# In step zero, VectorE instead of ScalarE copies queries, keys and kept rows out of PSUM

## What is computed

```python
def _adj_from_feats(Xa, W1, W2, W3):
    Q = Xa @ W1
    K = Xa @ W3
    logits = Q @ W2 @ K.T / TAU
    idx = jnp.argsort(-logits, axis=1)
    ...
    keep_sorted = ranks < k_i[:, None]      # k_i: entries until the sum passes 0.9
    ...
    masked = jnp.where(keep, logits, -jnp.inf)
    return jax.nn.softmax(masked, axis=1)
for s in range(STEPS):                       # STEPS = 2
    A = _adj_from_feats(Xa, W1, W2, W3)
    Xf = Rf @ Xf
    Xb = Rb @ Xb
    Xa = A @ Xa
    Z = Z + (Xf @ U1[s] + Xb @ U2[s] + Xa @ U3[s])
Y = X + Z
```

## Time and profile before

| what | us |
|---|---|
| three runs: median (lowest, highest) | 2160.16 (2159.7, 2162.64) |
| profiled execution: time, and its span | 2161.51, 2159.80 |
| busy in the span: PE, PEld | 1879.6, 1255.7 |
| busy in the span: DVE, ACT, POOL | 1911.5, 1681.3, 945.7 |
| mean granted TensorE clock, as a share of 2.4 GHz | 0.953 |

### The profile page before, as it was taken

One profiled execution on the slowest core, in us unless ns is written; L12 is line 12 of the kernel. 1 busy time (PEld: TensorE's weight loads), 2 busy tenths in 40 slices (PEclk: granted clock), 3 DMA queues, 4 the chain that ended last, 5 costly groups with the idle time before them and its releaser, 6 DMA issues. The chain is left out here.

```text
span 2159.8 us, 32672 instructions
## 1 busy us (share of the span) xinstructions
PE 1879.6 (87%) x9866; PEld 1255.7 (58%) x9866; DVE 1911.5 (89%) x6117; ACT 1681.3 (78%) x1740; POOL 945.7 (44%) x1542
## 2 busy tenths in 40 slices
PE   3999765999999999999973999989998999899892
PEld 2565433666666666666641656565656666565662
DVE  7788888999999999999748999999999999999995
ACT  5444256999999999999626898999998998999840
POOL 2000054666666666666605344443444344434424
PEclk9999987999999999999996999999999999999996
DMA  7788330111111111111116010101010010101023
GB/s 263 294 317 312 119 131 20 34 55 51 56 56 40 49 55 51 56 56 50 40 64 220 1 45 23 45 23 45 23 44 24 26 42 23 45 23 45 22 95 122
DMA packets 65727, 167.62 MB, mean 78 GB/s; under 512 B 7037, under 2 KB 45307, under 8 KB 61947
## 3 DMA queue, kind: packets, MB, share of 16 engines
q1 hardware_dynamic: 65530, 165.43, 22.1%
HBM read 117.95 MB, written 47.45 MB: 77 GB/s over the span
## 5 line engine op out<-in xcount | busy, mean ns | idle before, releaser
L1474 PE MATMUL banks<-xa,pt 128*128 128x256 f32 x2704 | 642.7, 389 | 7.6 <-ACT pt L974 7.6
L1474 PEld LDWEIGHTS banks<-xa,pt 128*128 128x128 f32 x2704 | 507.7, 194 | 146.6 <-issue 71.3
L946 ACT ACTIVATE junk_a<-pb_all,minus_t 128x3327 f16<-128x3327 f32 x150 | 460.7, 3071 | 73.8 <-POOLq L866 71.6
L950 ACT ACTIVATE junk_a<-pb_all,minus_t 128x3327 f16<-128x3327 f32 x150 | 460.6, 3071 | 4.1
L1525 PE MATMUL banks<-region,at 128*128 128x512 f16 x2028 | 456.1, 380 | 0.0
L850 POOL TENSOR_SCALAR over<-over,target 128x1 f32<-128x1 f32 x150 | 219.3, 1462 | 269.8 <-ACT junk_a L946 267.3
L1525 PEld LDWEIGHTS banks<-region,at 128*128 128x128 f16 x2028 | 196.6, 98 | 218.0 <-issue 2.0
L1400 PE MATMUL banks<-keys,qs 64*128 64x512 f32 (+1 forms) x816 | 192.0, 568 | 91.7 <-DMA qs<-q_d 31.9
L974 ACT ACTIVATE pt<-banks 128x896 f32<-128x896 f32 x208 | 173.2, 859 | 75.1 <-PE banks L1466 74.2
L1266 DVE TENSOR_SCALAR_CACHE_REDUCE pb_all<-banks 128x1024 f32<-128x1024 f32 x260 | 209.2, 848 | 21.3 <-PE banks L1400 13.0
L1128 DVE MAX8 junk_v<-below 128x8 f32<-128x208 f32 (+1 forms) x624 | 222.4, 432 | 2.2
(11 more groups left out here) (224 smaller groups left out, 2835.0 us busy)
## 6 DMA issues: line engine op xcount, KB each, us to landing
at<-adjT_d SPq DMA_DIRECT2D x52, 832.0 KB, 4.8
region<-in_adj_dram SPq DMA_DIRECT2D x25, 1663.5 KB, 7.9
adjT_d<-at SPq DMA_DIRECT2D x26, 832.0 KB, 3.9
fb_d<-fb_sb SPq DMA_DIRECT2D x26, 256.0 KB, 2.0
region<-fb_d SPq DMA_DIRECT2D x2, 3328.0 KB, 19.2
y_d<-y_sb SPq DMA_DIRECT2D x50, 128.0 KB, 1.7
x_d<-pb_all SPq DMA_DIRECT2D x1, 3328.0 KB, 10.4
qs<-q_d SPq DMA_DIRECT2D x104, 32.0 KB, 4.1
```

The costliest lines, as they stand in the source:

```text
L946: nc.scalar.activation(junk_a[:, 0:w], pb[u][:, 0:w], ACT.Relu, scale=sign, bias=t, accum_out=over[u][:, a:a + 1])\
L950: nc.scalar.activation(junk_a[:, 0:w], pb[u][:, 0:w], ACT.Sign, scale=sign, bias=t, accum_out=over[u][:, 2 + a:3 + a])\
L1474: last = nc.tensor.matmul(bank[4][:, 0:D], pt[sl][:, t * P:(t + 1) * P], xa[:, t0 + t, :], start=(t0 + t == 0), stop=(t0 + t == T - 1))
```

## The change

Step one is untouched. In step zero three things move from ScalarE to VectorE. The copies of queries and keys (ScalarE's `queries_keys`, behind its last copy of transposed pieces) go into `add_z`, behind the sum of z. With this `add_z` no longer waits for `qk_done`, and its first copy waits for the store of `qo` of the tile before. The kept rows of tile i - 1 become `kept_rows(i - 1)`, between the release of `unsettled` and the masking pass of tile i; for the last tile they stand in VectorE's iteration for i = 26, in front of the takes of step one's first scores. TensorE's, POOL's and SP's orders are as before.

```diff
@@ ScalarE, body(i) @@
-                    def queries_keys(q):
-
-                        act.wait_ge(S("z_psum"), q.n + 1)
-                        act.wait_ge(S("qo_stored"), 16 * q.n)
-                        nc.scalar.activation(qo[:, :], bank[7][0:DA, D:D + P], ACT.Copy)
-                        nc.scalar.activation(key_tiles(1, q.t, 1), bank[7][DA:2 * DA, D:D + P], ACT.Copy)\
-                            .then_inc(S("qk_done"), 1)
-
...
-                        if first and c == NT - 1 and (k + -1).inside(T):
-                            queries_keys(k + -1)
...
-                    if k.inside(T):
+                    if not first and k.inside(T):
 
                         sl, use = k.ring(NT, NT - 1)
                         act.wait_ge(S2("pt_used")[sl], use + 1)
-                        if first:
-                            act.wait_ge(S2("xo_stored")[k.slot], 16 * k.use)
                         nc.scalar.activation(xo_sb[k.slot][:, :], bank[4][:, 0:D], ACT.Copy, scale=rkept[k.slot][:, :])\
                             .then_inc(S2("xo")[k.slot], 1)
@@ VectorE, search(i) @@
                     dve.sem_inc(S("unsettled"), 1)
                     if first:
+                        kept_rows(i + -1)
                         ch.add(nc.vector.scalar_tensor_tensor(out=p, in0=p, scalar=left_max[:, :], in1=p, op0=ALU.is_gt, op1=ALU.mult))
@@ VectorE, add_z(k) @@
                         dve.wait_ge(S("z_psum"), k.n + 1)
-                        dve.wait_ge(S("qk_done"), k.n + 1)
                         dve.wait_ge(S2("y_stored")[k.slot], 16 * k.use)
                         nc.vector.tensor_tensor(y_sb[k.slot][:, :], bank[7][:, 0:D], xa[:, k.t, :], ALU.add).then_inc(S2("y_done")[k.slot], 1)
+                        dve.wait_ge(S("qo_stored"), 16 * k.n)
+                        nc.vector.tensor_copy(qo[:, :], bank[7][0:DA, D:D + P])
+                        nc.vector.tensor_copy(key_tiles(1, k.t, 1), bank[7][DA:2 * DA, D:D + P]).then_inc(S("qk_done"), 1)
...
+                def kept_rows(k):
+
+                    if not k.inside(T):
+                        return
+                    sl, use = k.ring(NT, NT - 1)
+                    dve.wait_ge(S2("pt_used")[sl], use + 1)
+                    dve.wait_ge(S2("xo_stored")[k.slot], 16 * k.use)
+                    nc.vector.tensor_scalar(xo_sb[k.slot][:, :], bank[4][:, 0:D], rkept[k.slot][:, :], None, ALU.mult)\
+                        .then_inc(S2("xo")[k.slot], 1)
@@ VectorE, body(i), iterations 26 and 27 @@
                         spread(i + -1)
                         add_z(i + -2)
+                        if first:
+                            kept_rows(i + -1)
                         if first and i.t == T:
                             take_logits(nxt, 0, 3)
```

## The result

The changed kernel takes **2188.46 us** in the median of four runs (2184.68 to 2190.25), against 2159.93 us for the kernel before on the same chip (2159.01 to 2162.64). The ratio is 1.0128, 95% interval 1.011 to 1.0145: slower by 1.3%. The forecast was 2176.3 us with a range up to 2184, so the sign was right and the size was not: +28.5 us where the sum said +16.1. The profiled execution has a time of 2188.08 and a span of 2186.4 us, 26.6 us over the 2159.8 of before.

The account below looks back on a forecast made before the run. VectorE was taken to bound step zero's tiles. Steady part +17.3, tile 1 +0.2, tile 24 to 25 -2.3 and step zero's end +0.9 gave +16.1 us on a 2160.16 median: 2176.3 us, range 2166 to 2184.

Parts of the forecast that it names:

- What bounds the tile: Step zero's steady tiles: VectorE has no idle time from L1077 to the mask, so work added there lengthens the 29.357 us period.
- Hidden work: Rival: the new work hides in VectorE's 1.6 us wait in front of L1077, only end terms stay; 2159 us, chance 0.12.
- ScalarE's pace: Rival: VectorE's start hangs on ScalarE's last sum, so freed ScalarE time pulls it forward; 2148 us, chance 0.07.
- The copies: Query and key copies behind VectorE's sum of z: 0.53 us a tile, 0.65 us for keys of tile 13 and later.
- What is given back: From mask to next L1077: POOL's chain loses a step, returning 0.16 to 0.36 us a tile, taken as 0.20.
- The floor of 5.31 us: Mask to next L1077: VectorE's own branch allows no less than 5.31 us, in place of 5.47.
- Tile 24: Tile 24 to 25: POOL's L864 goes ahead of the later mask, -3.35 us; with tile 25's later mask together -2.3 us.
- The takes of step one's scores behind the kept rows: End of step zero: the takes queue behind the kept rows, +0.5 us; with last copies' +0.4 us, together +0.9 us.
- the kept rows: Ahead of VectorE's masking pass: 0.41 us a tile, lower bound 0.33, their two waits met in a normal tile.
- the third rival: Nothing is given back: mask to next L1077 stays 5.47 us, steady cost 21.8 us; 2182 or 2185 us, chance 0.16.
- nobody downstream gains a start: Steady tiles: ScalarE's moved work, 0.54 and 0.47 us, precedes longer waits of 1.37 and 0.55 us, so ScalarE only gains idle time.
- The last sentence of the text on record: Sign of being wrong: period stays 29.4 us, falls, or another engine, above all TensorE, shows a new wait in each tile.

Follow-up runs that it names:

- e4: Kernel before with two copies and one product that nobody reads added on VectorE in step zero, nothing taken from ScalarE: 2185.01 us, ratio 1.0106.
- e9: Kernel before with the query and key copies moved to VectorE for one tile alone, those standing in tile 24: 2159.30 us, ratio 0.9988.
- e13: Kernel after with 20 unread transposes added on TensorE in one place, ahead of the transposes of tile 25: 2187.06 us, ratio 1.0120.
- e2: Kernel after with the query and key copies back on ScalarE, so only the kept rows are moved to VectorE: 2179.07 us, ratio 1.0082.
- e3: Kernel after with eight unread transposes on TensorE ahead of its wait for the masked rows in each step-zero tile: 2180.16 us, ratio 1.0085.
- e5: Kernel before with eight unread transposes on TensorE ahead of its wait for the masked rows in each step-zero tile: 2160.86 us, ratio 0.9999.
- e6: Kernel before with eight unread transposes on TensorE in each tile of both steps: 2159.40 us, ratio 0.9995.
- e8: Kernel before with only the kept rows moved to VectorE, issued behind the masking pass after the flag's load: 2222.05 us, ratio 1.0281.

## Why the prediction was wrong

Right, by its own steps:

- **What bounds the tile.** VectorE's chain does, and added work there counts nearly in full. Hidden work (2159) and ScalarE's pace (2148) are out: e4, without any relief, costs nearly the same (1.0106 and 1.0128).
- **The copies.** 0.53 and 0.65 us were forecast. From the sum of z to the next MAX8 there are now 0.83 us instead of 0.34 (tiles 2 to 14) and 0.95 from tile 15 on: 0.50 and 0.61 us. The step for the later keys, taken from one row, is there. MAX8 follows the key copy by 0.21 us in the tile shown above and by 0.33 from tile 15 on (802.18 to 802.51). The Trainium skill (VectorE: DVE Perf Modes, section "Two Vector instructions with no wait between them") has this as its rule, and the trace agrees.
- **What is given back.** 0.20 forecast; mask to next pass is 5.25 us in the mean instead of 5.47, so 0.21 to 0.22. L850 and L852 changed roles as written. The floor of 5.31 us was none, though: six of the 22 tiles have 5.11.
- **Tile 24.** -3.35 forecast, -3.34 measured, for the named reason: with a later mask POOL's L864 goes ahead of it. A later mask alone does that (e4), and e9 shows it in one tile. That the two numbers agree to 0.01 us is luck, since the same instructions gave -3.61 in e13.
- **The takes of step one's scores behind the kept rows.** L1417 waits for one take at 1134.65, and the last copies cost 0.4 us (from L1446 to the last L1417 1.67 us, where it was 1.30).

Slightly mis-sized: the kept rows. 0.41 forecast, 0.47 measured (e2: first pass to mask 24.36 instead of 23.89 in the tiles with a first pass of 3.68 us). From L1252 to the mask there are 0.40 us, as taken; the other 0.07 us lie in front of it, behind the release of `unsettled`, where L1252 starts after 0.22 us of idle time. Further, in 15 of the 22 tiles of e3 the first pass takes about 3.84 instead of 3.68 us, since POOL's L899, 0.40 us, now starts some 0.03 us ahead of it. The Trainium skill (SBUF — State Buffer, section "Who interferes with whom") lets the first to start win. The trace agrees in the order: 0.16 us for VectorE here, less than the 0.37 us that L899 still had to run, and 3.5 us for POOL where VectorE was first (L850, 3.79 us in the earlier trace rows and 0.29 above). These make the period with the clock kept 30.27 us, where the forecast's mean was 30.14: 2.9 us over 22 tiles. The sums of the third rival were about 1 us too high: its own terms, with the 0.9 of the end, give 2181 and 2184 us and not 2182 and 2185. Both lie below what was measured.

**The step that failed** is in the first part, "nobody downstream gains a start", and in the sum that follows from it: I added VectorE's extra time to a tile in which every other engine keeps its speed. I asked who would be released earlier, and not who would now be idle longer. TensorE's wait for the masked rows grew from about 1 to about 2 us, and behind it the clock fell in 7 of 22 tiles (5.3 us) and at tile 25 (2.7 us, e13). The measured share agrees: with the waits filled (e3) the span is 8.0 us shorter, 4.7 of it in tiles 2 to 24 and 3.0 in the end. The four runs of the kernel after point the same way: their times go with their mean granted clock, 2184.68 us at 0.950, 2188.08 and 2188.84 at 0.946, 2190.25 at 0.942. The row that could have told it was in the trace of before. In step one TensorE waits 1.24 and 0.84 us and is then at 0.51 for 3.4 us, and something like it stands in 12 of 26 tiles, while step zero's waits of 0.75 to 1.22 us had no fall behind them in tiles 2 to 23. The change made step zero's waits about as long as those of step one. The last sentence of the text on record names the place ("TensorE ... shows a new wait in each tile"), but it gave it neither a price nor a chance, and the range ended at 2184 for that reason. The rows of before told that such falls occur; what one costs in step zero they did not tell, since in step one it costs nothing.

So the 26.6 us between the spans are 17.3 of the forecast's steady part, 2.9 of sizes in VectorE's tile, 4.7 of long tiles, 2.7 of the clock at tile 25, -3.3 and +1.8 at tile 24 and in the rest of the end (forecast -3.35 and +1.96), and 0.5 for the stage ahead, tiles 0 and 1 and step one. The medians differ by 28.5; their own spread of 3 to 6 us covers the rest.

**What stays open:** which tiles fall. A wait of 1.76 us had a fall behind it in e2 and one of 2.48 us had none in the kernel after, and at tile 25 the same wait went both ways (e5, e6). The runs show that the falls make the long tiles and that in tiles 2 to 23 they stand behind the longer waits, not when one comes.

## What to carry to other kernels

When work is put on the engine that sets the pace, ask of each engine that waits for it how long it will now be idle, and if that is TensorE, look in the trace for the waits behind which its clock already falls; then see whether TensorE has a wait further on that can take up the loss; where it has none, and an engine without slack waits for its result, give such a fall a price and a chance. Test it with work that nobody reads in that wait: in the steady tiles it cost nothing here (e5), and it separates the clock from other causes. Read every stage of its trace, since it can move a fall to another place, and take more than one execution where the clock may or may not fall. An engine's idle time is a place for work only if the result is not needed sooner, which e8 paid for with 60 us.
